# Dense branches of the early groups moved behind the late ones in the second routing, their residual rows stored ahead of it

## The reference, cut to what matters

```python
xn = layernorm(x) * ln_gamma + ln_beta
abel_out = gelu(xn @ abel_w + abel_b)            # the dense branch
logits = xn @ moe_gate_w + moe_gate_b            # 8 experts, the best 2 are kept
topw, topi = top_k(logits, 2); topw = softmax(topw)
h = gelu(xn @ ew1[e] + eb1[e]); eo = h @ ew2[e] + eb2[e]     # for the chosen experts
moe_out = (weighted sum of eo) @ expm(gens[0]) @ expm(gens[1]) @ expm(gens[2])
gate = sigmoid([abel_out, moe_out] @ gc_w + gc_b)
out = x + abel_out * (1 - gate) + moe_out * gate
```

## Time and profile before

| what | us |
|---|---|
| median of 3 executions | 1418.49 |
| lowest, highest | 1414.60, 1419.76 |
| the profiled execution, its own time | 1422.55 |
| its span in the profile | 1420.9 |
| PE busy in it (share) | 1180.7 (83%) |
| DVE, ACT, POOL busy | 862.8, 495.4, 411.6 |

### The profile page before, as it was taken

One profiled execution on the slowest core, in us unless ns is written; L12 is line 12 of the kernel. 1 busy time (PEld: TensorE's weight loads), 2 busy tenths in 40 slices (PEclk: granted clock), 3 DMA queues, 4 the chain that ended last, 5 costly groups with the idle time before them and its releaser, 6 DMA issues.

```text
span 1420.9 us, 26058 instructions
## 1 busy us (share of the span) xinstructions
PE 1180.7 (83%) x7280; PEld 1022.1 (72%) x7281; DVE 862.8 (61%) x2756; ACT 495.4 (35%) x967; POOL 411.6 (29%) x480
## 2 busy tenths in 40 slices
PE   6796876955599999992699998999883799999958
PEld 5664555854488989992588987888772688998947
DVE  6435766744456666665676658766536456666646
ACT  1111551332244444441233333343342334444435
POOL 3001101566134444441000000104454244444420
PEclk9897995877899999996899999999896799999989
DMA  9400231446474333335011011001157663343357
GB/s 288 145 0 7 83 119 52 153 149 215 152 237 120 90 91 89 91 87 208 0 46 45 1 45 46 1 1 56 71 217 244 198 226 103 105 135 103 106 173 249
DMA packets 75727, 161.73 MB, mean 114 GB/s; under 512 B 11302, under 2 KB 36594, under 8 KB 75642
## 3 DMA queue, kind: packets, MB, share of 16 engines
q1 hardware_dynamic: 55082, 105.45, 21.5%
q0 software_dynamic: 19776, 54.45, 12.5%
q10 hardware_dynamic: 784, 0.79, 0.2%
HBM read 88.92 MB, written 71.73 MB: 113 GB/s over the span
## 4 chain that ended last, share of the span: by engine, by line
PE 52%; issue 12%; DVE 6%; DMA 3%; ACT 3%; another core or an unknown queue 3%; POOL 3%; POOLq 1%; SPq 1%; DVEq 0%; ACTq 0%
PE bank L2077 15%; PE bank L1621 6%; PE bank L1622 6%; PE bank L1490 6%; PE bank L1623 6%; PE bank L1647 3%; PE bank L1700 2%; DMA xh<-slots_in 2%; PE bank L2135 2%; POOL xh L1301 2%; PE bank L1630 2%; PE bank L1533 1%; PE bank L186 1%; POOLq L1300 1%
## 5 line engine op out<-in xcount | busy, mean ns | idle before, releaser
L1621 PE MATMUL bank<-ew,rows 128*128 x852 | 298.4, 350 | 4.3 <-DVE rows L1175 2.6
L1622 PE MATMUL bank<-low_in,rows 128*128 x852 | 273.3, 321 | 0.0
L1623 PE MATMUL bank<-ew,rows 128*128 x852 | 272.8, 320 | 0.0
L1312 POOL DMA_INDIRECT results<-xh x142 | 141.8, 998 | 295.7 <-DVE xh L1203 277.5
L1621 PEld LDWEIGHTS bank<-ew,rows 128*128 128x128 f32 x852 | 161.8, 190 | 15.3 <-issue 8.2
L1623 PEld LDWEIGHTS bank<-ew,rows 128*128 128x128 f32 x852 | 161.4, 189 | 12.2
L1622 PEld LDWEIGHTS bank<-low_in,rows 128*128 128x128 f32 x852 | 162.5, 191 | 6.0
L1457 ACT ACTIVATE xh<-bank 128x512 f32<-128x512 f32 x142 | 85.0, 599 | 219.4 <-PE bank L1623 219.4
L1212 DVE TENSOR_TENSOR rows<-bank,rows 128x512 fp32r<-128x512 f32 x142 | 98.3, 692 | 96.1 <-ACT rows L198 82.1
L1291 POOL DMA_INDIRECT slots_in<-xh,work x120 | 117.1, 976 | 101.2 <-DVE work L1071 67.6
L634 POOL TENSOR_TENSOR work<-work,mhalf 128x8 f32<-128x8 f32 (+1 forms) x22 | 38.7, 1760 | 332.7 <-DVE work L627 332.6
(11 more groups left out here) (334 smaller groups left out, 2037.5 us busy)
## 6 DMA issues: line engine op xcount, KB each, us to landing
xh<-slots_in POOLq DMA_DIRECT2D x142, 129.0 KB
low_in<-low SPq DMA_DIRECT2D x32, 512.0 KB
xh<-results SPq DMA_DIRECT2D x14, 1032.0 KB, 5.2
residual<-xs SPq DMA_DIRECT2D x16, 512.0 KB
dense<-ab SPq DMA_DIRECT2D x16, 512.0 KB
xs<-residual SPq DMA_DIRECT2D x16, 512.0 KB
ab<-dense SPq DMA_DIRECT2D x9, 512.0 KB, 9.3
xs<-in_L_attn_a_x_dram SPq DMA_DIRECT2D x4, 1024.0 KB
```

Source lines behind the costliest of these rows:

```text
L1312: pool.indirect_dma_start(out=yg, out_offset=bass.IndirectOffsetOnAxis(ap=back[j % RING], axis=0), in_=yr[j % RING], in_offset=None).then_ ...
L1621: pe.matmul(o, hi, f32r(high(c)), start=(c == 0), stop=False)
L1622: pe.matmul(o, hi, f32r(low(c)), start=False, stop=False)
L1623: last = pe.matmul(o, lo, f32r(high(c)), start=False, stop=(stop and c == chunks[-1]))
```

## The change

At the second routing the order of the steps becomes 3, 4, 5, 6, 7, 0, 1, 2: the early groups' transposition, dense branch and gelu come after those of the late groups. PE forms the total of the counts at the sixth step (`total_rows`), not after all steps. SP stores the residual rows of groups 0, 1 and 2 at the start of its part (inside the attention's last rows, as soon as ACT has rewritten them), and fetches the weights of experts 0 and 1 after the pads, not within the steps. DVE forms three gates between the late groups and five after the tables, where it was four and four. The spill semaphores go by step, not by group. The first routing stays as it is.

```diff
--- before.py
+++ after.py
@@ -975,9 +975,8 @@
 
 
             EARLY_GROUPS = 3 if r == 1 else 0
-            ORDER = [3, 0, 4, 1, 5, 2, 6, 7] if r == 1 else list(range(NG))
+            ORDER = [*range(EARLY_GROUPS, NG), *range(EARLY_GROUPS)]
             step_of = {g: p for p, g in enumerate(ORDER)}
-            assert all(step_of[g] < step_of[g + 4] for g in range(NG - 4))
             if r == 0:
                 place = [xh[:, tiles(g), :] for g in range(NG)]
             else:
@@ -1100,7 +1099,7 @@
                                     ALU.subtract).then_inc(rest_ok, 1)
 
 
-                LATE = {NG - 4: (0,), NG - 3: (1,), NG - 2: (2, 3)} if r == 0 else {NG - 3: (0,), NG - 2: (1,), NG - 1: (2, 3)}
+                LATE = {NG - 4: (0,), NG - 3: (1,), NG - 2: (2, 3)} if r == 0 else {NG - 3: (0,), NG - 2: (1,), NG - 1: (2,)}
                 assert NG == 8
                 if r == 0:
                     then(v, v.memset(run[0], 0.0))
@@ -1159,7 +1158,7 @@
                 then(v, v.tensor_scalar(wts[:, :, 0], dtop, 1.0, None, ALU.add))
                 then(v, v.reciprocal(wts[:, :, 0], wts[:, :, 0]))
                 then(v, v.tensor_tensor(wts[:, :, 1], dtop, wts[:, :, 0], ALU.mult))
-                for p in range(NG // 2, NG):
+                for p in range(NG // 2 if r == 0 else NG // 2 - 1, NG):
                     dense_gate(ORDER[p])
                     if r == 0:
                         rest_late(1 + p - NG // 2)
@@ -1314,17 +1313,21 @@
 
             def sync(sp):
 
+                def spill_residual(g):
+                    sp.wait_ge(res_ok, GT * (g + 1))
+                    sp.dma_start(xs_out[g], xs[:, tiles(g), :].rearrange("p t c -> p (t c)")).then_inc(spilled[step_of[g] % 4], 16)
+
                 def spill(p):
                     g = ORDER[p]
-                    sp.wait_ge(res_ok, GT * (g + 1))
-                    sp.dma_start(xs_out[g], xs[:, tiles(g), :].rearrange("p t c -> p (t c)")).then_inc(spilled[g % 4], 16)
+                    if g >= EARLY_GROUPS:
+                        spill_residual(g)
                     sp.wait_ge(gelu_ok, p + 1)
-                    sp.dma_start(ab_out[g], ab[:, tiles(g), :].rearrange("p t c -> p (t c)")).then_inc(spilled[g % 4], 16)
+                    sp.dma_start(ab_out[g], ab[:, tiles(g), :].rearrange("p t c -> p (t c)")).then_inc(spilled[p % 4], 16)
 
                 def fetch_weights(e):
                     after(sp, low_ld, WEIGHTS * e)
 
-                    sp.wait_ge(spilled[e % 4], 32 * (e // 4 + 1 if r == 0 else 2))
+                    sp.wait_ge(spilled[step_of[e] % 4], 32 * (step_of[e] // 4 + 1 if r == 0 else 2))
                     sp.wait_ge(zab_ok, GT * (step_of[e] + 1))
                     sp.dma_start(low1_in[:, e].rearrange("p c h -> p (c h)"), low1[e]).then_inc(low_ld, 16)
                     sp.dma_start(low2_in[:, e].rearrange("p h c -> p (h c)"), low2[e]).then_inc(low_ld, 16)
@@ -1341,13 +1344,16 @@
                     if n % 2:
                         sp.dma_start(high2[e].rearrange("p (h c) -> p h c", h=HC), ew2[:, :, e, :]).then_inc(late_high, 16)
 
+
+                for g in range(EARLY_GROUPS):
+                    spill_residual(g)
                 for p in range(NG):
                     if r == 0 and p == NG // 2 + 1:
                         sp.wait_ge(att_ps, NG)
                         sp.dma_start(late_R.rearrange("p c j -> p (c j)"), turning).then_inc(turning_ld, 16)
                     spill(p)
-                    if 0 <= p - (3 if r == 0 else 5) < EARLY:
-                        fetch_weights(p - (3 if r == 0 else 5))
+                    if r == 0 and 0 <= p - 3 < EARLY:
+                        fetch_weights(p - 3)
                 if r == 0:
                     store_fold(0)
 
@@ -1357,6 +1363,8 @@
                     sp.dma_start(xg[bass.ds(at, P), :], zero[:]).then_inc(padded, 16)
                 for n in range(1, LATE_FOLDS):
                     store_fold(n)
+                for e in range(EARLY if r == 1 else 0):
+                    fetch_weights(e)
                 sp.wait_ge(x_ld[RING - 1], 16)
                 if r == 0:
                     sp.wait_ge(late_high, 16 * LATE_FOLDS // 2)
@@ -1566,6 +1574,11 @@
                     attend(0)
                     attend(1)
                     attend(2)
+                def total_rows():
+                    pe.wait_ge(run_ok, NG)
+                    pe.wait_ge(lg_ok, NG)
+                    pe.matmul(bank[:, 6, 0:E], onesb[:], run[NG % 2], start=True, stop=True).then_inc(rank_ps, 1)
+
                 chosen = []
                 for p in range(NG + 1):
                     routed = p < NG and ORDER[p] >= EARLY_GROUPS
@@ -1585,15 +1598,16 @@
                         chosen.append(ORDER[p])
                     if p == 1:
                         dense(0)
+                    if p == NG - EARLY_GROUPS and r == 1:
+                        total_rows()
                 if r == 0:
                     pe.wait_ge(x1_ok, 2 * NG)
                     pe.wait_ge(turning_ld, 16)
                     turn_late(0)
                     fold_late(0)
                     turn_late(1)
-                pe.wait_ge(run_ok, NG)
-                pe.wait_ge(lg_ok, NG)
-                pe.matmul(bank[:, 6, 0:E], onesb[:], run[NG % 2], start=True, stop=True).then_inc(rank_ps, 1)
+                if r == 0:
+                    total_rows()
                 pe.wait_ge(xT_ok, NG)
                 pe.wait_ge(gelu_ok, NG)
                 for e in range(E):
```

## The result

The changed kernel took 1428.88 us (median of 10, 1425.06 to 1433.97), the kernel before 1417.59 (10, 1413.36 to 1423.80). The ratio is 1.0077, 95% interval 1.0063 to 1.0092: **slower by 11 us**, where 12 us less were forecast. The profiled execution took 1425.63 (span 1424.0), that of before 1422.55 (span 1420.9). The first is 3 us under its median and the second 5 over its own, so I compare stretches, not spans. DVE's last row of the attention started at 1012.2 (before: 1016.1), the second expert loop at 1116.25 (before: 1110.02). The routing between them has grown from 93.9 to 104.0 us, by 10.1: that is the loss.

A forecast was written before the change was run, and what follows sets the result against it. SP's queue, reaching its pads late after the last gelu, was taken to bound the second expert loop's start. 1110.0 - 1097.7 - 0.5 = 11.8, rounded to 12, gave 1406.5 us against the median, range 1398 to 1414.

The forecast's parts named there:

- part 2: Second routing in the new order: tables from 1060, last gelu ends 1075 (1072.5 to 1079), POOL's scatters end 1080.
- Rival D: Second routing: PE's clock stays lower without the early groups as filler, last gelu after 1087.5; 1429.5 us, chance 0.06.
- Part 1: Three early residual spills (1.5 MB) go into SP's 147.7 us wait in the attention; cost and gain by themselves 0.
- Part 3: SP after the last gelu: eight pads start at 1075.4 and take 14.4 us (8.7 to 16.3), done at 1089.8.
- rival B: Pads quick in an empty queue, 8.7 in place of 14.4 us; 18 us gained, 1400.5 us, chance 0.27.
- Tile path: From the end of SP's pads through the first tile to the second expert loop: 7.9 us, giving 1097.7.
- Weight path: Fetch of expert 0's weights, issued at 1090 behind the pads and no longer hidden: 7.5 us, giving 1097.5.
- Gates: DVE's five gates of 1.9 us behind the last gelu end by 1087, covered ahead of the loop's start at 1097.7.
- The loop: Second expert loop: one more weight fetch, that of expert 1, runs beside it and costs 0.5 us.
- The sum: Loop start moved from 1110.0 to 1097.7, less 0.5 in the loop: 11.8 us gained, rounded to 12.

The follow-up runs named there:

- e6: The kernel before, order of steps kept, with the weight fetches of experts 0 and 1 moved behind the pads; ratio 0.9991 on chip B.
- b1: The kernel before, unchanged, run for its profile on chip A; 1369.17 us.

## Why the prediction was wrong, step by step

**The step that failed** is in part 2: "Now and then ACT waited for PE with no reason that I can name, 4.18 us at 1051.56; I add 2." On chip R these waits make the last gelu 28.5 us later than on chip A (83.9 against 55.4), and with that the gain turns into a loss. I treated a wait without a name as noise with a mean. It had a cause in the kernel, and the change multiplied it. Its partner is the sentence on POOL: scatters "begin for group 4 near 1039 and then follow each other: end 1080 ... so they are off the path". The end came out (1080.64), in part by luck, since the whole routing began 3.9 us earlier than in the trace it was read from; "follow each other" was right, and that is the train of sixteen. I asked only whether POOL's own end was late, not what the train does to others. The trace of before had more than the one wait. In the second routing ACT's timeline has another, 6.35 us without a releaser until 1063.39, beside the train from 1054.9 to 1064.7. In its first routing, where trains of sixteen are the rule, ACT's timeline has:

```profile
286.18 1.02 ACT L203 ACTIVATE work<-bank 128x1024 f32<-128x1024 f32 x1 [8.92 <-remote]
...
324.71 0.20 ACT L198 ACTIVATE work<-bank 128x32 f32<-128x32 f32 x1 [14.28 <-remote]
```

8.92 and 14.28, with POOL's trains at 271.8 to 291.9 and 301.7 to 321.9. That was the price of the new order, in a stretch that I read only for the pads. On chip A, which has no late results, no wait of ACT in 260 to 330 is over 5.20.

**The rival that got the number.** Rival D's 1429.5 is what was measured (1428.88), and its condition, a last gelu later than 1087.5, was met (1096.1). Its cause was not, so the match is a coincidence. It wanted every dense branch at 6.54 from the start; the second and third ran at 5.62 and 5.38 with logits, clock 1.00, and with the scatters away it is 0.97 over the 45 us of the window. The rule of the Trainium skill behind it (TensorE: Matmul & The Clock Gate, "Why this matters for your kernels": no idle gaps between bursts) shows here as an after-effect only: after the wait of 8.79 us the next dense branch took 6.50 instead of 3.69. Behind the shorter waits a logits step took 2.59 instead of 1.69, a transposition 1.95 instead of 1.07, a dense branch 5.01 instead of 3.69. Together that is some 6 of the 28.5 us.

**Point by point**, with chip A for what the steps were worth without late results:

- Part 1, residual rows: forecast 0, alone 0.9995. Right.
- Part 2 without the unnamed waits: the tables were forecast 44 us behind DVE's last row (1060 - 1016) and came at 43.9; the last scatter 63, came at 63.3; the last gelu's end 59, with a low end of 56.5, came at 56.4 (start 55.4). Right, a little too cautious.
- Part 3, pads: I took 14.4, with 8.7 as the low end. They took 8.25 on R and 8.60 on A, the price of rival B. The 14.4 came from a place with scatters still running (and the two times that it was read from are 14.7 apart). Behind the train there are none: the same eight pads took 14.28 and 15.19 us beside a train on R and B (before, e6), and 9.63 beside one on A (b1), which has no late results. The term was mis-sized, by the same effect.
- Tile path: forecast 7.9; from the last pad (issued 1106.21, by the chain of waits) to the loop (1116.25) it took 10.0 us, against 8.2 in the earlier trace rows. The first tile took 3.84 instead of 2.36 beside the weights. Two us too low.
- Weight path: forecast 7.5, 7.3 from 1106.65 to 1113.96; no longer the last. Right.
- Gates: forecast to end 12 us behind the last gelu, ended 12.0 behind it (1109.1), ahead of the loop. Covered here as forecast; not once the pads move forward.
- The loop: from its start to the end of the span 307.8 us against 310.9. No cost seen.

The sum on chip A: loop at 76.3, forecast 81.7 (1097.7 - 1016). Yet the gain is 8.3 and not 12: the kernel before starts its loop 9.3 us earlier on A than on R (84.6 against 93.9), and the forecast was 5.4 too late for the changed one. Two errors of the sum work against each other there.

## What to carry to other kernels

A wait whose releaser the profile cannot name is a term of the sum: find every such wait in the trace, see what they have in common, and ask what the change does to that. A reordering that packs the producers of an asynchronous engine closer also joins its bursts; cost a burst by what it does to the others, not only by when it ends. And a gain of under one per cent that depends on such waits has to be timed on more than one chip.

## What the runs showed of the hardware

- During an uninterrupted train of indirect scatters issued by POOL (16 in 20 us), other engines see PE's results up to 13.35 us after their modelled end, PE's matmuls of 0.2 us come 0.7 to 2.1 us apart, and SP's eight pads take 14 to 17 us instead of 8 to 10 (14.28, 15.19, 16.52 and 16.80 on R, B, B and F). DVE's own sequence of tables inside the second train (1068.26 to 1074.8) ran without such a gap. Trains of eight delay too, by 4 to 7 us (4.18 and 6.35 on R, 4.60 and 6.87 on E).
- This shows on R, B, E and F (three or four chips) and not at all on three (A, C, D), with the same program. The kernel before takes 1410 to 1418 us on the first and 1369 to 1371 on the others; 44.6 of the 54.5 us between R and A lie ahead of the first expert loop and in the second routing. Only A was used at two separate times, without late results at both, so that it is a property of the chip is likely and not shown. Why it differs, whether it is the completion signals or the supply of instructions that is late, and whether the number of scatters outstanding or their sheer rate decides, stays open: no run took these apart.
